# Gates multiplied straight out of the PSUM bank, norms moved to VectorE, a reciprocal built from Ln and Exp on ScalarE

## The chip, the cores and the metric

The kernel is one program on one core of a Trainium2 chip. The metric is the device time of one execution, in microseconds. Five engines work side by side, each through its own queue in order: TensorE (PE; its weight loads are listed as PEld), VectorE (DVE), ScalarE (ACT), GpSimd (POOL) and SyncE (SP), which here issues the transfers. They meet through semaphores.

## The reference

Two transformer-like layers work on `x` of shape 8 x 512 x 256. Layer 0 is a state-space block and a gated MLP, layer 1 a cumulative attention and a mixture of experts. Each of the four parts is followed by `layernorm(x + part(x))`. Cut to what matters here:

```python
# layer 0, state space: 512 channels, 128 states, one step per position
h = exp(dt_t * A) * h + dt_t * B_t * u_t ;  y_t = h . C_t
y = y * rsqrt(mean(y*y) + eps) * norm_w ;  y = y * silu(z) ;  out = y @ out_proj
# layer 0, MLP
h = silu(x@w1 * s1) * (x@w2 * s2) ; h = gelu(h@h1) ; h = gelu(h@h2) ; out = h@w3
# layer 1, attention, its input under one more rms_norm (no weight)
q, k, v = split(rms_norm(x) @ w_qkv) ; q, k = rms_norm(q), rms_norm(k)
w = cumsum(exp(k)) ; kv = cumsum(exp(k) * v)
y = sigmoid(q) * kv / (w + 1e-6) ; u, g = split(y @ w_swiglu) ; out = x + (u * silu(g)) @ w_out
# layernorm(x) = (x - mean) / sqrt(var + 1e-5)
```

## The kernel before, in words

Three phases follow one another: a projection phase (the inputs of the recurrence, written to memory), `stream_phase` (the recurrence, with all of layer 0's rest and the attention mixed in) and `expert_phase`. The change is in `stream_phase` alone.

`stream_phase` cuts the 512 positions into 8 chunks of 64 (all 8 sequences at once). Stage c, one call of `body(c, m, last)` on every engine, runs the recurrence of chunk c; beside it the engines work on chunk m = c - 1: layer 0 of that chunk and the attention of the chunk before it. Stage 0 has nothing beside the recurrence, stage 1 only layer 0. After stage 7 a tail works off the last chunk, with wider use of the banks.

The recurrence has 256 slots n = 0..255 per stage (position t = n // 4, two sequences each), paired as k = n // 2 = 0..127:

- GpSimd multiplies the state by the decay (L1612) in slot n, after VectorE's add of slot n - 4 and after the decay of k is ready.
- ScalarE makes the decay of k + 3 in its turn k (`exp_pool`, L1264, from rows that SyncE fetched) and VectorE's share of it (`exp_dve`, L1269, in place in a bank, after TensorE's L884).
- VectorE adds the input term in slot n (L1650), after GpSimd's product of slot n and TensorE's outer product (L870), and in even slots multiplies its own share (`keep`, L1640).
- TensorE waits in slot n for the add of slot n, then issues the outer product of slot n + 2, then the mixed-in product of slot n, if there is one, and after odd slots reads the state out (L896).

The mixed-in work stands in tables of slots. TensorE has one bank, `bank[:, M0]`, for all mixed-in products: each must be read before the next is written. `bank_read` waits for whoever frees the one before (`FREED_BY`). `GATE_AT` = 44, 48, .. 72 and `UP_AT` = 46, 50, .. are the eight pairs of gate and up products of the MLP, `Z_AT` = 1, 3, 5, 7 the four z products, `SWI_AT` = 174, 176, 188, 189 the four of the attention's gate.

For a gate, ScalarE copies the product out of the bank in the turn that covers its slot (`copy_gate`, L1332, with the scale s1), which frees the bank, and takes tanh of half the copy (`tanh_gate`, L1337). VectorE forms (tanh + 1) * copy three slots after the product (`silu_gate`, L1692) and multiplies it with the up product in the slot after that one (`hidden`, L1698). z (`copy_z` L1309, `tanh_z` L1313, `silu_z` L1671) and the attention's gate (`copy_swi` L1407, `tanh_swi` L1411, `silu_swi` L1748) go the same way.

For a layernorm, VectorE takes mean and variance (L1656, L1660), ScalarE the root as exp(-0.5 ln(var + eps)) (`root`, L1280 to L1283, which loads its table set explicitly each time), VectorE forms a shift (`spread`, L1665), and ScalarE applies scale and shift (`normed`, L1304), four tiles of 128 x 256. The extra rms_norm in front of the attention is made by ScalarE from the normed x: four squares (L1353), a root, four scalings (`to_unit`, L1359). The reciprocal of the attention's denominator is VectorE's (L1737), two of 128 x 512 per chunk.

VectorE and ScalarE take this work in program order with the recurrence: a mixed-in instruction that waits holds back the adds or the decays behind it.

## Time and profile before

| | |
|---|---|
| Median of the three timed runs (5382.38 to 5397.47) | 5395.41 us |
| Profiled execution, its own time | 5389.25 us |
| Its span | 5387.5 us |
| Granted TensorE clock over the span | 0.888 of full speed |
| Busy time: PE, DVE, ACT, POOL | 4718.6, 3855.4, 3391.4, 4011.9 us |
| Stages 0 to 7 of the stream (first to last L1612) | 316.8 to 4308.6 us |
| Tail of the stream | 4308.6 to 4636.5 us |

Times in the rows are microseconds from the start of the span, durations microseconds or, where marked so, nanoseconds; TensorE's busy time is modelled and says little of how near it is to its peak. Idle time of an engine is given with what released it.

### The profile page before, as it was taken

How to read it: one execution, taken by the hardware profiler on the slowest of the kernel's cores; microseconds unless marked ns; L12 is line 12 of the kernel's file. 1: busy time of each engine (PE TensorE's matmuls, PEld its weight loads, DVE VectorE, ACT ScalarE, POOL GpSimd, SP SyncE). 2: the span in 40 equal slices, each digit the busy share in tenths (PEclk: the TensorE clock that was granted, in tenths of full speed). 3: DMA queues.
4: the chain of work that ended last, by engine and by line, in shares of the span. 5: the costliest groups of instructions: out<-in, count | busy, mean ns of one | idle time of the engine just before them, and what ended most of it. 6: DMA issues, size and time to landing. Idle time of an engine off the chain costs nothing. (4 is left out here: it accounts for less than half of the span.)

```text
span 5387.5 us, 69474 instructions
## 1 busy us (share of the span) xinstructions
PE 4718.6 (88%) x21278; PEld 1827.4 (34%) x21278; DVE 3855.4 (72%) x4448; ACT 3391.4 (63%) x4022; POOL 4011.9 (74%) x2364
## 2 busy tenths in 40 slices
PE   8669998998999899989988998999899978569998
PEld 4301112223222222322222222222322334458886
DVE  6868888888988898879889987898898830500012
ACT  6646666777777877787777777777877643111112
POOL 0079998998999899989989998999899900243332
PEclk9855558998999999999999998999999989589999
DMA  3367766776777677767776776777677712245445
GB/s 112 123 212 262 246 239 227 272 263 235 253 249 271 237 256 254 270 220 251 261 263 232 264 261 243 247 261 266 242 252 265 257 51 63 77 166 179 176 176 184
DMA packets 316759, 1189.59 MB, mean 221 GB/s; under 512 B 77296, under 2 KB 115056, under 8 KB 305392
## 3 DMA queue, kind: packets, MB, share of 16 engines
q1 hardware_dynamic: 293456, 1070.18, 57.3%
q0 software_dynamic: 22944, 114.98, 6.1%
q8 instruction: 182, 2.98, 0.2%
q14 instruction: 177, 1.45, 0.1%
HBM read 1129.61 MB, written 89.19 MB: 226 GB/s over the span
## 5 line engine op out<-in xcount | busy, mean ns | idle before, releaser
L1612 POOL TENSOR_TENSOR s_h<-s_decay,s_h 128x768 f32<-128x768 f32 x2048 | 3708.8, 1852 | 282.8 <-ACT s_decay L1264 272.9
L1650 DVE TENSOR_TENSOR s_h<-s_h,bank 128x1024 f32<-128x1024 f32 x2048 | 2470.2, 1216 | 394.2 <-POOL s_h L1612 210.9
L1264 ACT ACTIVATE s_decay<-s_decay,s_a_neg 128x1536 f32<-128x1536 f32 x1024 | 1606.5, 1569 | 231.3 <-DMA s_decay<-dt_rows 229.8
L896 PE MATMUL bank<-s_h,s_cdiag 128*32 128x512 f32 x8192 | 1251.7, 687 | 10.8 <-ACT s_y L1276 10.7
L1269 ACT ACTIVATE bank<-bank,s_a_neg 128x512 f32<-128x512 f32 x1024 | 672.4, 657 | 637.3 <-PE bank L884 633.8
L870 PE MATMUL bank<-s_vrow,s_brow 9*128 9x512 bf16 x4096 | 844.6, 421 | 260.0 <-DVE s_h L1650 228.5
L870 PEld LDWEIGHTS bank<-s_vrow,s_brow 9*128 9x128 bf16 x4096 | 209.0, 92 | 1480.3 <-issue 1477.1
L1640 DVE TENSOR_TENSOR s_h<-bank,s_h 128x512 f32<-128x512 f32 x1024 | 699.8, 683 | 3.4 <-ACT bank L1269 3.1
L1008 PE MATMUL bank<-m_mb,m_w 128*128 128x512 f32 x1024 | 518.0, 635 | 1.4 <-ACT m_mb L1342 1.4
L994 PE MATMUL bank<-m_ma,m_w 128*128 128x512 f32 x1024 | 517.1, 634 | 0.0
L884 PE MATMUL bank<-s_drow,s_unit 3*128 3x512 bf16 x1024 | 432.2, 423 | 76.4 <-DMA s_drow<-dt_parts 46.9
L2204 ACT ACTIVATE e_hid<-bank 128x512 f32<-128x512 f32 x156 | 93.3, 598 | 454.2 <-PE bank L2063 454.2
L896 PEld LDWEIGHTS bank<-s_h,s_cdiag 128*32 128x32 f32 x8192 | 169.5, 114 | 403.8 <-issue 385.7
L2063 PE MATMUL bank<-e_pj,e_hid 128*128 128x256 f32 x1248 | 278.7, 381 | 12.0 <-issue 12.0
L2063 PE MATMUL bank<-e_cT,e_fc 128*128 128x256 f32 x1248 | 278.4, 382 | 0.8 <-DVE e_cT L2389 0.8
L884 PEld LDWEIGHTS bank<-s_drow,s_unit 3*128 3x128 bf16 x1024 | 96.4, 94 | 493.6 <-issue 471.1
L2063 PEld LDWEIGHTS bank<-e_pj,e_hid 128*128 128x128 f32 x1248 | 233.9, 190 | 50.5 <-issue 20.3
L2063 PEld LDWEIGHTS bank<-e_cT,e_fc 128*128 128x128 f32 x1248 | 238.9, 191 | 34.1 <-issue 1.2
L994 PEld LDWEIGHTS bank<-m_ma,m_w 128*128 128x128 f32 x1024 | 181.2, 194 | 200.6 <-issue 200.5
L1008 PEld LDWEIGHTS bank<-m_mb,m_w 128*128 128x128 f32 x1024 | 180.7, 194 | 198.1 <-issue 195.9
L2000 POOL MEMSET e_eps<- 128x1 f32 x1 | 0.1, 98 | 327.7 <-POOLq L2498 327.7
L2389 DVE COPY e_cT<-bank 128x256 f32<-128x256 f32 x39 | 16.6, 425 | 299.9 <-PE bank L2123 299.9
(229 smaller groups left out, 4096.5 us busy)
## 6 DMA issues: line engine op xcount, KB each, us to landing
s_decay<-dt_rows SPq DMA_DIRECT2D x1024, 768.0 KB, 5.6
m_w<-in_units SPq DMA_DIRECT2D x210, 512.0 KB, 5.5
s_vrow<-v_parts SPq DMA_DIRECT2D x1024, 36.0 KB
slots<-in_fill SPq DMA_DIRECT2D x512, 64.5 KB, 4.5
s_brow<-b_parts SPq DMA_DIRECT2D x1024, 9.0 KB
v_parts<-p_part SPq DMA_DIRECT2D x24, 512.0 KB, 3.0
m_w<-w_scaled SPq DMA_DIRECT2D x16, 512.0 KB, 4.9
e_got<-expert_out SPq DMA_DIRECT2D x8, 1024.0 KB, 7.1
```

What stands on the lines that cost most here:

```text
L870: mm = pe.matmul(bank[:, X0 + n % 2 * PAIR + b], brow[q:q + PAIRS, buf, hf, at * STATE:(at + 1) * STATE], vrow[q:q + PAIRS, buf, hf, at * ...
L884: pe.matmul(bank[:, E0 + hf], unit[q:q + PARTS], drow[q:q + PARTS, buf, t % STEPS], start=True, stop=True).then_inc(e_ps, 1)
L896: mm = pe.matmul(bank[q * 32:(q + 1) * 32, Y0], cdiag[:, hf * LANES + q, at * BLK:(at + 1) * BLK], h[:, t % 2, hf * LANES + q], start=(at ...
L994: mm = pe.matmul(bank[:, j % 4 if tail else M0], w[:, slot, k * P:(k + 1) * P], ma[:, k], start=(k == 0), stop=(k == KH - 1))
L1008: mm = pe.matmul(bank[:, j % 4 if tail else M0], w[:, slot, k * P:(k + 1) * P], mb[:, k], start=(k == 0), stop=(k == KH - 1))
L1264: act.activation(decay[:, k % RING], decay[:, k % RING], ACT.Exp, scale=a_neg[:, 1:2]).then_inc(decay_ok, 1)
L1269: act.activation(bank[:, E0 + k % HALVES], bank[:, E0 + k % HALVES], ACT.Exp, scale=a_neg[:, 1:2]).then_inc(e_ok, 1)
L1612: pool.tensor_tensor(h[:, t % 2, g * PAIR:(g + 1) * PAIR, DCOLS:], decay[:, k % RING, g % 2 * PAIR:(g % 2 + 1) * PAIR], h[:, (t + 1) % 2, ...
L1640: dve.tensor_tensor(h[:, t % 2, hf * LANES:(hf + 1) * LANES, 0:DCOLS], bank[:, E0 + hf].rearrange("p (b d) -> p b d", b=LANES), h[:, (t + ...
L1650: dve.tensor_tensor(h[:, t % 2, g * PAIR:(g + 1) * PAIR], h[:, t % 2, g * PAIR:(g + 1) * PAIR], bank[:, X0 + n % 2 * PAIR:X0 + (n % 2 + 1) ...
L2063: mm = pe.matmul(dst, lhs(k), rhs(k), start=(k == 0), stop=(k == n - 1))
L2204: act.activation(hid[:, r, 2 * m:2 * m + 2].rearrange("p m t -> p (m t)"), bank[:, m], ACT.Gelu).then_inc(up_ok, 1)
```

## The change

- z, gate and attention gate are no longer copied out of the bank. ScalarE takes the tanh from the bank (for the gate with scale 0.5 * s1), and VectorE forms (tanh + 1) * bank. The s1 of the copy goes into the constant of `hidden`, 0.5 * s1 * s2. The bank is now freed by VectorE's product, so `FREED_BY` names `z_ok`, `g_ok2` and `sg_ok`.
- VectorE's product stands one slot after TensorE's: `SILU_Z_AT` 2, 4, 6, 8; `SILU_GATE_AT` 45, 49, .. 73; `SILU_SWI_AT` 175, 177. Two up products move (63 to 62, 71 to 70).
- `spread`, its shift and ScalarE's `normed` go. VectorE applies (x - mean) * rstd with a tensor_scalar on four tiles per norm, at slots 36 to 39, 155 to 164 and 211 to 214.
- The four squares of the extra rms_norm go: its root is taken from the layernorm's variance, since rstd * rms of the normed x is 1 / sqrt(var * (1 + eps_rms) + eps_ln * eps_rms). `root_x` now stands ahead of `root_var` of norm 1, both in ScalarE's turn 0, and VectorE makes the unit x from the raw x (`unit_x`, slots 3 to 6).
- The two reciprocals go; ScalarE takes Ln of both denominators, then Exp of minus that (`invert`, turn 60). The denominators are formed at 112 and 116 instead of 114 and 124.
- Behind three of the sixteen Gelus the Ln-and-Exp set is loaded explicitly. The root of norm 0 moves from turn 16 to 17, that of norm 2 from 103 to 104.

```diff
-UP_AT = (46, 50, 54, 58, 63, 66, 71, 74)
+UP_AT = (46, 50, 54, 58, 62, 66, 70, 74)
...
-FREED_BY = {"z": ("z_free", TT), "xn": ("xn_ok", KD), "qk": ("qk_cp", TT), "gT": ("gT_ok", KI), "o": ("o_add", 2),
-"kT": ("ew_ok", KD), "qT": ("eq_ok", KD), "v": ("kv_ok", KD), "xt": ("xt_ok", KD), "gate": ("g_free", KH),
+FREED_BY = {"z": ("z_ok", TT), "xn": ("xn_ok", KD), "qk": ("qk_cp", TT), "gT": ("gT_ok", KI), "o": ("o_add", 2),
+"kT": ("ew_ok", KD), "qT": ("eq_ok", KD), "v": ("kv_ok", KD), "xt": ("xt_ok", KD), "gate": ("g_ok2", KH),
...
-SILU_Z_AT = (4, 5, 8, 10)
-SILU_GATE_AT = (47, 51, 55, 59, 63, 67, 71, 75)
-SILU_SWI_AT = (180, 183)
-ROOT_AT = (16, 0, 103)
-SPREAD_AT = (35, 3, 210)
-ROOT_X_AT = 2
+SILU_Z_AT = (2, 4, 6, 8)
+SILU_GATE_AT = (45, 49, 53, 57, 61, 65, 69, 73)
+SILU_SWI_AT = (175, 177)
+ROOT_AT = (17, 0, 104)
+NORM_AT = ((36, 37, 38, 39), (155, 158, 161, 164), (211, 212, 213, 214))
+UNIT_X_AT = (3, 4, 5, 6)
+LOG_NEXT = (("h1", 4), ("h2", 5), ("h2", KH - 1))
...
-DEN_AT = (114, 124)
-REC_AT = (121, 131)
+DEN_AT = (112, 116)
+INVERT_AT = 60
...
-NORM_1_AT = {2: (0, 1, 2, 3)}
-X_SQ_AT = {2: (0, 1, 2, 3)}
-TO_UNIT_AT = {2: (0,), 3: (1, 2, 3)}
...
-NORM_0_AT = {17: (0,), 18: (1, 2, 3)}
-NORM_2_AT = {106: (0,), 108: (1, 2, 3)}
...
-        pe.wait_ge(S("sg_free"), FIRST + m * KD + i - 1)
+        pe.wait_ge(S("sg_ok"), FIRST + m * KD + i - 1)
...
-def root(m, mean, dst, eps, ln_sem, ok_sem):
+def root(m, mean, dst, eps, ln_sem, ok_sem, scale=1.0):
...
-    act.activation(dst, mean, ACT.Ln, bias=eps).then_inc(ln_sem, 1)
+    act.activation(dst, mean, ACT.Ln, bias=eps, scale=scale).then_inc(ln_sem, 1)
...
 def root_x(m):
-    act.wait_ge(S("xsq"), FIRST + (m + 1) * TT)
-    root(m, sm[:, 8:12], sm[:, 12:16], eps_rms, S("xrs_ln"), S("xrs_ok"))
+    act.wait_ge(S("mv_ok", 1), FIRST + (m + 1) * TT)
+    root(m, mv[:, 1, :, 1], sm[:, 12:16], eps_both, S("xrs_ln"), S("xrs_ok"), 1.0 + RMS_EPS)
...
 def root_qk(m):
-def normed(m, n, i, src, dst):
-    act.wait_ge(S("sh_ok", n), FIRST + m + 1)
-    act.activation(dst[:, i], src[:, i], ACT.Identity, scale=rstd[:, n, i:i + 1],
-                   bias=shift[:, n, i:i + 1]).then_inc(S("lnx", n), 1)
-def copy_z(m, i, tail):
+def tanh_z(m, i, tail):
...
-    act.activation(sz[:, i], bank[:, i if tail else M0], ACT.Copy).then_inc(S("z_free"), 1)
-def tanh_z(m, i):
-    act.wait_ge(S("z_free"), FIRST + m * TT + i + 1)
-    act.activation(ma[:, KI + i], sz[:, i], ACT.Tanh, scale=0.5).then_inc(S("z_th"), 1)
+    act.activation(ma[:, KI + i], bank[:, i if tail else M0], ACT.Tanh, scale=0.5).then_inc(S("z_th"), 1)
...
-def mean_square_x(m, i):
-    act.wait_ge(S("lnx", 1), FIRST + m * TT + i + 1)
-    act.activation(xn2[:, i], x2[:, i], ACT.Square, scale=DIM ** -0.5, accum_out=sm[:, 8 + i:9 + i]).then_inc(S("xsq"), 1)
-def to_unit(m, i):
-    if i == 0:
-        act.wait_ge(S("xrs_ok"), FIRST + m + 1)
-        act.wait_ge(S("out_ok"), FIRST + m)
-    act.activation(xn2[:, i], x2[:, i], ACT.Identity, scale=sm[:, 12 + i:13 + i]
-                   ).then_inc(S("xr_ok"), 1)
...
-def copy_swi(m, i, tail):
+def invert(m):
+    act.preload_act_table_set("natural_log_exp_and_others")
+    for c in range(KD):
+        act.wait_ge(S("den_ok"), FIRST + m * KD + c + 1)
+        act.activation(data(qk_runs[:, c]), data(qk_runs[:, c]), ACT.Ln).then_inc(S("rec_ln"), 1)
+    for c in range(KD):
+        act.wait_ge(S("rec_ln"), FIRST + m * KD + c + 1)
+        act.activation(data(qk_runs[:, c]), data(qk_runs[:, c]), ACT.Exp, scale=-1.0).then_inc(S("rec_ok"), 1)
+def tanh_swi(m, i, tail):
...
-    act.activation(u[:, i], bank[:, 4 + i if tail else M0], ACT.Copy).then_inc(S("sg_free"), 1)
-def tanh_swi(m, i):
-    act.wait_ge(S("sg_free"), FIRST + m * KD + i + 1)
-    act.activation(qk[:, i], u[:, i], ACT.Tanh, scale=0.5).then_inc(S("sg_th"), 1)
+    act.activation(qk[:, i], bank[:, 4 + i if tail else M0], ACT.Tanh, scale=0.5).then_inc(S("sg_th"), 1)
...
 def out_of_bank(m, n, attn):
-        copy_z(m, Z_AT.index(n), False)
-        tanh_z(m, Z_AT.index(n))
+        tanh_z(m, Z_AT.index(n), False)
...
-        copy_gate(m, GATE_AT.index(n), False)
-        tanh_gate(m, GATE_AT.index(n))
+        tanh_gate(m, GATE_AT.index(n), False)
...
-        copy_swi(m - 1, SWI_AT.index(n), False)
-        tanh_swi(m - 1, SWI_AT.index(n))
+        tanh_swi(m - 1, SWI_AT.index(n), False)
...
+            if ("h1", j) in LOG_NEXT:
+                act.preload_act_table_set("natural_log_exp_and_others")
...
+            if ("h2", j) in LOG_NEXT:
+                act.preload_act_table_set("natural_log_exp_and_others")
...
 def aside(m, k, attn):
+        root_x(m - 1)
...
-    if attn and k in NORM_1_AT:
-        for i in NORM_1_AT[k]:
-            normed(m - 1, 1, i, x2, x2)
-    if attn and k in X_SQ_AT:
-        for i in X_SQ_AT[k]:
-            mean_square_x(m - 1, i)
-    if attn and k == ROOT_X_AT:
-        root_x(m - 1)
-    if attn and k in TO_UNIT_AT:
-        for i in TO_UNIT_AT[k]:
-            to_unit(m - 1, i)
...
-    if k in NORM_0_AT:
-        for i in NORM_0_AT[k]:
-            normed(m, 0, i, xa, xa)
-    if attn and k in NORM_2_AT:
-        for i in NORM_2_AT[k]:
-            normed(m - 1, 2, i, x2, xn2)
+    if attn and k == INVERT_AT:
+        invert(m - 1)
...
-def spread(m, n):
+def normed(m, n, i, src, dst):
...
-    dve.scalar_tensor_tensor(out=shift[:, n], in0=mv[:, n, :, 0], scalar=-1.0, in1=rstd[:, n], op0=ALU.mult,
-                             op1=ALU.mult).then_inc(S("sh_ok", n), 1)
-def silu_z(m, i):
+    if n == 1:
+        dve.wait_ge(S("xr_ok"), FIRST + (m + 1) * TT)
+    if n == 2 and i == 0:
+        dve.wait_ge(S("out_ok"), FIRST + m)
+    dve.tensor_scalar(dst[:, i], src[:, i], mv[:, n, i, 0:1], rstd[:, n, i:i + 1], ALU.subtract, ALU.mult
+                      ).then_inc(S("lnx", n), 1)
+def unit_x(m, i):
+    if i == 0:
+        dve.wait_ge(S("xrs_ok"), FIRST + m + 1)
+        dve.wait_ge(S("out_ok"), FIRST + m)
+    dve.tensor_scalar(xn2[:, i], x2[:, i], mv[:, 1, i, 0:1], sm[:, 12 + i:13 + i], ALU.subtract, ALU.mult
+                      ).then_inc(S("xr_ok"), 1)
+def silu_z(m, i, tail):
...
-    dve.scalar_tensor_tensor(out=sz[:, i], in0=ma[:, KI + i], scalar=1.0, in1=sz[:, i],
+    dve.scalar_tensor_tensor(out=sz[:, i], in0=ma[:, KI + i], scalar=1.0, in1=bank[:, i if tail else M0],
...
-def silu_gate(m, j):
+def silu_gate(m, j, tail):
...
-    dve.scalar_tensor_tensor(out=mb[:, j], in0=ma[:, j], scalar=1.0, in1=mb[:, j], op0=ALU.add,
-                             op1=ALU.mult).then_inc(S("g_ok2"), 1)
+    dve.scalar_tensor_tensor(out=mb[:, j], in0=ma[:, j], scalar=1.0, in1=bank[:, j % 2 * 2 if tail else M0],
+                             op0=ALU.add, op1=ALU.mult).then_inc(S("g_ok2"), 1)
...
 def hidden(m, j, tail):
-                             scalar=half_s2[:, j:j + 1], in1=mb[:, j], op0=ALU.mult, op1=ALU.mult
+                             scalar=half_s12[:, j:j + 1], in1=mb[:, j], op0=ALU.mult, op1=ALU.mult
...
 def add_attended(m, pair, tail):
+    dve.wait_ge(S("lnx", 1), FIRST + (m + 1) * TT)
...
 def mix(m, n, attn):
-    if attn and n == SPREAD_AT[1]:
-        spread(m - 1, 1)
...
-        silu_z(m, SILU_Z_AT.index(n))
+        silu_z(m, SILU_Z_AT.index(n), False)
+    if attn and n in UNIT_X_AT:
+        unit_x(m - 1, UNIT_X_AT.index(n))
...
-    if n == SPREAD_AT[0]:
-        spread(m, 0)
+    if n in NORM_AT[0]:
+        normed(m, 0, NORM_AT[0].index(n), xa, xa)
+    if attn and n in NORM_AT[1]:
+        normed(m - 1, 1, NORM_AT[1].index(n), x2, x2)
...
-        silu_gate(m, SILU_GATE_AT.index(n))
+        silu_gate(m, SILU_GATE_AT.index(n), False)
...
-for i in range(TT):
-    normed(end, 0, i, xa, xa)
...
+invert(end - 1)
...
-    copy_gate(end, j, True)
-    tanh_gate(end, j)
+    tanh_gate(end, j, True)
...
-for i in range(TT):
-    normed(end - 1, 2, i, x2, xn2)
...
+root_x(end)
...
-for i in range(TT):
-    normed(end, 1, i, x2, x2)
-for i in range(TT):
-    mean_square_x(end, i)
...
+invert(end)
...
-for i in range(TT):
-    normed(end, 2, i, x2, xn2)
...
```

## Rows read from the trace of the kernel before

**Rows 1.** page, costliest groups: count, busy us, mean ns, idle before them us and its releasers

```profile
L1612 POOL TENSOR_TENSOR s_h<-s_decay,s_h 128x768 f32<-128x768 f32 x2048 | 3708.8, 1852 | 282.8 <-ACT s_decay L1264 272.9
L1650 DVE TENSOR_TENSOR s_h<-s_h,bank 128x1024 f32<-128x1024 f32 x2048 | 2470.2, 1216 | 394.2 <-POOL s_h L1612 210.9
```

**Rows 2.** groups by line, GpSimd alone: stage 0 (316.8 to 773.1), stage 6 (3301.1 to 3807.2)

```profile
L1612 POOL TENSOR_TENSOR s_h<-s_decay,s_h 128x768 f32<-128x768 f32 x256 | 455.6, 1825 | 0.7 <-ACT s_decay L1264 0.4
...
L1612 POOL TENSOR_TENSOR s_h<-s_decay,s_h 128x768 f32<-128x768 f32 x257 | 467.8, 1857 | 40.1 <-ACT s_decay L1264 39.6 <-DVE s_h L1650 0.3
```

**Rows 3.** timeline around one gate: start us, duration us, instruction, idle before it

```profile
3422.63 1.21 DVE L1650 TENSOR_TENSOR s_h<-s_h,bank 128x1024 f32<-128x1024 f32 x1
3423.99 0.39 PE L870 MATMUL bank<-s_vrow,s_brow 9*128 9x512 bf16 x2 [0.82 <-DVE s_h L1650]
3424.31 1.98 PE L970 MATMUL bank<-m_cT,m_w 128*128 128x512 f32 x4
3426.33 0.69 ACT L1332 ACTIVATE m_mb<-bank,m_s 128x512 f32<-128x512 f32 x1 [1.98 <-PE bank L970]
3427.05 0.63 ACT L1337 ACTIVATE m_ma<-m_mb 128x512 f32<-128x512 f32 x1
3427.86 1.98 PE L980 MATMUL bank<-m_cT,m_w 128*128 128x512 f32 x4
3428.34 1.80 DVE L1692 SCALAR_TENSOR_TENSOR m_mb<-m_ma,m_mb 128x512 f32<-128x512 f32 x1
3430.18 0.75 DVE L1698 SCALAR_TENSOR_TENSOR m_ma<-bank,m_half_s,m_mb 128x512 f32<-128x512 f32 x1
3430.84 1.21 DVE L1650 TENSOR_TENSOR s_h<-s_h,bank 128x1024 f32<-128x1024 f32 x1
3432.52 1.98 PE L970 MATMUL bank<-m_cT,m_w 128*128 128x512 f32 x4
```

**Rows 4.** windows: all eight gates, busy us by engine, granted clock, DMA

```profile
3408.03:3472.16 64.13, 57.81 (x273) 16.63 (x273) 60.62 (x64) 45.85 (x52) 56.75 (x32) 1.00 0.69 238
```

**Rows 5.** groups by line and shape, whole trace: the fused multiply on two kinds of operands

```profile
L1748 DVE SCALAR_TENSOR_TENSOR m_u<-m_qk,m_u 128x512 f32<-128x512 f32 x16 | 27.6, 1728 | 9.9 <-ACT m_qk L1411 9.9
L1759 DVE SCALAR_TENSOR_TENSOR m_x<-m_x,bank 128x512 f32<-128x512 f32 x16 | 11.0, 687 | 14.9 <-PE bank L1103 14.9
```

**Rows 6.** timeline, opening of stage 6: table load, root, first tanh, GpSimd's stall

```profile
3310.12 1.21 DVE L1650 TENSOR_TENSOR s_h<-s_h,bank 128x1024 f32<-128x1024 f32 x1
3310.87 1.28 ACT L1280 ACT_TABLE_LOAD   x1
3312.17 0.30 ACT L1281 ACTIVATE m_rstd<-m_mv,m_const 128x4 f32<-128x4 f32 x1
3315.11 0.63 ACT L1313 ACTIVATE m_ma<-m_mb 128x512 f32<-128x512 f32 x1
...
3333.35 1.82 POOL L1612 TENSOR_TENSOR s_h<-s_decay,s_h 128x768 f32<-128x768 f32 x1 [7.84 <-ACT s_decay L1264]
```

**Rows 7.** timeline, VectorE, where the first norm's shift is formed

```profile
3389.80 0.16 DVE L1665 SCALAR_TENSOR_TENSOR m_shift<-m_mv,m_rstd 128x4 f32<-128x4 f32 x1 [0.64 <-ACT m_rstd L1283]
3391.65 1.21 DVE L1650 TENSOR_TENSOR s_h<-s_h,bank 128x1024 f32<-128x1024 f32 x1
```

**Rows 8.** groups by line and shape: VectorE's tensor_scalar elsewhere in this trace

```profile
L370 DVE TENSOR_SCALAR p_conv<-p_xpad,p_cw,p_cb 128x512 f32<-128x512 f32 x16 | 8.7, 542 | 19.6 <-ACT p_xpad L280 19.6
L2344 DVE TENSOR_SCALAR e_parts<-e_job,e_jobs,e_more 128x40 f32<-128x40 f32 x7 | 2.1, 306 | 0.0
```

**Rows 9.** timeline: a reciprocal in the stream and the two of the tail

```profile
3556.75 3.35 DVE L1737 RECIPROCAL m_qk<-m_qk 128x512 f32<-128x512 f32 x1
...
4381.75 6.55 DVE L1737 RECIPROCAL m_qk<-m_qk 128x512 f32<-128x512 f32 x2
```

**Rows 10.** timeline, ScalarE, the tail's opening

```profile
4320.80 1.28 ACT L1280 ACT_TABLE_LOAD   x1
4332.70 1.71 ACT L1359 ACTIVATE m_xn<-m_x,m_sm 128x256 f32<-128x256 f32 x4
```

More of the change, by code:

```diff
@@ L1837, in keys_tail @@
                 for c in range(KD):
-                    invert(m, c)
-                for c in range(KD):
                     divide(m, c)
@@ L1843, in output_tail @@
                 for c in range(KD):
-                    silu_swi(m, c)
+                    silu_swi(m, c, True)
                 for c in range(KD):
@@ L1862, in _ @@
                 statistics(end, 0, xa, S("o_add"), pair)
-            spread(end, 0)
+            for i in range(TT):
+                normed(end, 0, i, xa, xa)
             keys_tail(end - 1)
             for j in range(KH):
-                silu_gate(end, j)
+                silu_gate(end, j, True)
                 hidden(end, j, True)
@@ L1872, in _ @@
                 statistics(end, 1, x2, S("x2_ok"), pair)
-            spread(end, 1)
+            for i in range(TT):
+                unit_x(end, i)
+            for i in range(TT):
+                normed(end, 1, i, x2, x2)
             keys_tail(end)
```

79 lines of the change are left out of this document (35 added, 44 removed).

## The prediction

> **What bounds the kernel now.** I read the costliest groups first, then GpSimd stage by stage, then the timeline of one stage, instruction by instruction. The stream is GpSimd's chain of decays: 2048 products of 1.85 us [rows 1]. Stage 0, which has only the recurrence, takes 256 slots in 456.3 us, 1.78 us a slot, with next to no idle time; stage 6 takes 506.1 us for as many, with 40.1 us idle, 39.6 of it behind ScalarE's decays, and products lengthened from 1825 to 1857 ns, 257 x 0.032 = 8.2 us [rows 2]. So a stage with everything in it has some 50 us to win, seven stages (37 in stage 1) about 340. The lengthening comes when VectorE runs an instruction with two SBUF inputs: (tanh + 1) * copy takes 1728 ns in the mean where the same shape with one operand in a bank takes 687 [rows 5], and a GpSimd product beside it grows too.
>
> The other half of the reading is how far the chain can lean on the rest. GpSimd in slot n needs VectorE's add of slot n - 4. TensorE in slot n needs the add of slot n, and VectorE issues its adds and its mixed-in work in one order. So whatever makes VectorE wait between add n and add n + 1 also holds TensorE's product of n + 1. GpSimd runs on for at most three more slots, 5.35 us. A wait that recurs uses that up once and then costs its full length.
>
> **The gates, the largest term.** Eight gates take 64.13 us from the first to the product behind the last [rows 4], 8.02 per four slots. One round [rows 3]: add ends 3423.84, gate product 3424.31 to 3426.29, copy, tanh to 3427.68. Meanwhile VectorE adds freely, TensorE starts up at 3427.86, ends at 3429.84, VectorE multiplies (L1692, then L1698 at 3430.18), adds at 3430.84, and the next gate starts at 3432.52. Copy, tanh and L1692 lie beside the next two adds and the up product. After the change L1692 stands right behind the add of the next slot, takes its operand from tanh and must run before the add that lets TensorE start up. The round is then one chain: 0.47 from add to product, 1.98 product, 0.04, 0.69 tanh (as the copy, also out of the bank with a pointer scale), 0.04, 0.69 L1692 [rows 5], an add of 1.21 less 0.08 overlap, 0.47, 1.98 up, 0.1, 0.75 L1698, 1.21 less 0.08. Sum 9.47, against 8.02: 1.45 lost per gate, 8 x 1.45 = 11.6 us a stage. The table load ahead of the first tanh (1.28) moves ahead of its wait for TensorE, under the product: nothing. The slack of 5.35 us doesn't pay it: in this stage GpSimd is some 3 us ahead when the last round ends, and the first Gelu behind it, whose decay comes late from ScalarE, takes the lead back to the same level whatever it was. I take 11.6; the bounds are 0 (something I miss lets the adds run on) and 13.
>
> **The stage's opening.** Before, ScalarE's turn 2 holds four normed, four squares, a root and a scaling, and GpSimd stands 7.84 us [rows 6]; with the smaller stalls around it the first 16 slots lose 12.6 us. All of that work leaves ScalarE. But VectorE's product of the first z moves from slot 4 to 2, and ScalarE's queue in front of that tanh is now: two roots (each 1.28 load, 0.30, 0.20 and gaps, 1.9), a square 0.6, a load 1.3, the tanh 0.6. Counted from 3310.87 [rows 6] it ends at 3317.1. The add that ran at 3310.12 then runs at 3317.8, and GpSimd's eighth product waits for it till 3319.1, 5.4 us later than before. Three more z rounds are chains as the gates are: 0.47 + 1.98 + 0.6 + 0.7 + 0.4 (unit_x) + 1.2, some 5.5 us per two slots where GpSimd needs 3.6, less what lead there is. Worked through slot by slot, GpSimd's product 16 starts at 3340.9, before at 3342.4. I take 1 us saved, bounds 9.5 saved (only ScalarE counts) and 4 lost.
>
> **Norm 0.** The first normed on VectorE stands at slot 36 and waits for a root that moved one turn later. Before, VectorE waited 0.64 for its shift and the next-but-one add ran at 3391.65 [rows 7]. ScalarE would end the root at about 3393.2, so that add slips by 2.2 us, of which some is caught up before the first gate. Take 1.4 lost, bounds 0 and 3.
>
> **The new tensor_scalars.** Sixteen of 128 x 256 a stage. The nearest rows are 542 ns for 128 x 512 and 306 for 128 x 40 [rows 8]; between them I take 0.42. Three spreads (up to 0.97 in this stage, behind a GpSimd product) and two reciprocals of 3.35 [rows 9] leave VectorE, so its total falls. For GpSimd, fourteen two-input instructions go, about 2.3 of the 8.2 us a stage; each new one may hold it for between 0 and 0.42, I take 0.2, 3.2 us. Net 0.9 lost, bounds 2.3 won and 4.4 lost.
>
> The Trainium skill (SBUF — State Buffer, Who interferes with whom) says that a VectorE instruction with two SBUF inputs, or a tensor_scalar in a two-port mode, holds the port pair it shares with GpSimd, and the second to start fully blocks. The 1728 against 687 ns agree for the first kind; no row shows the second beside GpSimd, and by that rule it costs the whole bound of 0.42.
>
> **Reciprocals and invert.** A reciprocal delays one add by 3.35 us and TensorE's piece behind it by about 1.4 us, and the Gelu stalls that follow lose 0.4 to 0.9 each. ScalarE gets 3.8 us in turn 60 (a load and four instructions of 0.6), of which its slack of some 3 us and the free 1.5 us a turn hide all but 0.3. Net 1 saved, bounds 2 saved and 1.5 lost. Table loads per stage stay 41: one less at z, one more at invert, three explicit ones in place of three implicit.
>
> **Attention's gate and norm 2.** Slots 174 and 176 are two more chained rounds. VectorE's product there no longer takes 2.34 and 1.87 us later on, so most is caught up by slot 184, but TensorE's pieces slip by about 1.6 us into a Gelu that already stalls. 1.6 lost, bounds 0 and 4. ScalarE's four normed of norm 2 gone: 0.7 saved, bounds 0 and 1.5.
>
> **The tail.** Nothing covers it, so what leaves the chain counts. ScalarE's copies and tanhs of z ran ahead of a root at 4320.80, four normed, four squares, and the extra root, and the scalings at 4332.70 [rows 10]; now both norm roots go under the z products and unit_x runs beside the rest: the first turned x comes 10.8 us earlier. At the end chunk the same again in serial, 6. The reciprocals were 6.55 each time [rows 9]; a load, which can go ahead, and Ln and Exp of 0.6 overlapping leave 2.8 and 4 saved. Copies ahead of tanh and the last spread and normed: 2.4. Sum 26 saved, bounds 12 and 32.
>
> **Sum.** A full stage: 11.6 - 1 + 1.4 + 0.9 - 1 + 1.6 - 0.7 = 12.8 lost, six of them 77. Stage 1 (no attention): 11.6 less 2 of z work, about 10. Tail -26. Together +61 on the profiled execution's 5389.25, 5450. The runs' median of 5395.41 stands 6 above that execution: 5456.
>
> **The rivals.** (1) The lead covers the chained rounds and only ScalarE's load counts. For it: 39.6 of 40.1 us of idle time are put down to ScalarE. Against it: in [rows 4] VectorE is busy 60.62 of 64.13 us and GpSimd only 56.75, so there it is no longer GpSimd that sets the pace. Per stage 9.5 at the opening, 8 x 0.6 at the gates (the copy), 1 at the reciprocals, 1 at each of the last two: 17 saved, six times, 8 in stage 1, 26 in the tail: 5259. It decides if VectorE's wait for tanh is under the time to its next add, 0.1 us, and I count 1.4. (2) The rounds cost half of 1.45 because up or the adds overlap more than one trace shows, and the opening saves 4: 5456 - 7 x 5.8 - 6 x 3 = 5397, no change. (3) The tensor_scalars hold GpSimd for their whole 0.42 and VectorE waits for the product that runs, up to 1.8 each, so that norm 0 and the unit_x round lose another 3: 3.5 + 3 per stage, six times 39: 5495. It decides where VectorE's own lead is gone, as at slots 36 to 39. (2) and the forecast differ in size, (1) in sign. The rule of the Trainium skill quoted above would put (3) at its full price.
>
> **How the numbers follow.** Forecast 0.66, rival (1) 0.13, (2) 0.11, (3) 0.10. The likeliest case alone spans 5415 to 5485. The range that leaves 2 in 10 out runs from 5385, inside rival (2), to 5500. A measurement here tells about 0.3%, 16 us, from no change. Faster: (1) and a corner of (2), 0.15; same: most of (2), 0.10; slower 0.75.
>
> **What would show it.** Right: the distance from one gate's first product to the next is 9.3 to 9.7 us; VectorE's L1692 counterpart shows idle time behind tanh; TensorE's outer products wait more for VectorE; GpSimd's idle time moves from ScalarE's decays to VectorE's adds and grows in slots 50 to 80; full stages take some 519 us; the tail is 300 us long. Wrong: rounds of 8 us or less there (the gate step falls), no stall near slot 7 or 8 (the opening), tensor_scalars with a mean over 1 us or GpSimd's mean over 1.87 (the locks).

## The result, and the profile after

The changed kernel takes 5589.51 us (median of 4 runs, 5582.65 to 5597.83) against 5388.90 us of the kernel before beside it (5380.50 to 5397.47): 1.037 times as long, 95% interval 1.0347 to 1.0392. The direction was forecast, the size was not: 61 us more were forecast, 201 came. The profiled execution took 5597.83 us, the longest of the four; its granted clock was 0.873 where it had been 0.888.

The page's costliest groups answer [rows 1] (count, busy us, mean ns, idle before them):

```profile
L1561 POOL TENSOR_TENSOR s_h<-s_decay,s_h 128x768 f32<-128x768 f32 x2048 | 3702.3, 1843 | 521.2 <-ACT s_decay L1260 389.4
L866 PE MATMUL bank<-s_vrow,s_brow 9*128 9x512 bf16 x4096 | 862.3, 428 | 437.7 <-DVE s_h L1601 406.9
```

GpSimd works as long as before, its products are even a little shorter, but it stands idle 521.2 us instead of 282.8: the whole loss is waiting. Half of the growth is put down to ScalarE's decays (272.9 to 389.4 us), half to VectorE's adds (8.7 to 125.4 us). GpSimd alone, grouped by line, in stages 0 and 6 [rows 2]:

```profile
L1561 POOL TENSOR_TENSOR s_h<-s_decay,s_h 128x768 f32<-128x768 f32 x257 | 457.3, 1825 | 2.0 <-ACT s_decay L1260 1.1 <-PE bank L892 0.8
...
L1561 POOL TENSOR_TENSOR s_h<-s_decay,s_h 128x768 f32<-128x768 f32 x258 | 468.9, 1851 | 67.2 <-ACT s_decay L1260 49.3 <-DVE s_h L1601 16.6 <-PE bank L892 0.8
```

Stage 3 cut at slots 0, 16, 44, 80, 136, 172 and 256, first the kernel before, then the changed one. The columns are the stretch and its length, busy us (count) of PE, PEld, DVE, ACT and POOL, the granted clock, DMA share, GB/s:

```profile
1775.86:1816.76 40.90, 30.23 (x125) 7.71 (x117) 29.80 (x31) 37.47 (x62) 29.10 (x18) 0.75 0.67 238
1816.76:1872.91 56.15, 49.36 (x275) 18.74 (x273) 48.74 (x58) 48.61 (x78) 51.61 (x28) 0.97 0.69 232
1872.91:1944.71 71.80, 64.70 (x309) 18.99 (x307) 67.26 (x71) 51.33 (x61) 65.06 (x38) 1.00 0.69 243
1944.71:2057.03 112.32, 102.18 (x471) 28.46 (x470) 104.37 (x94) 81.20 (x80) 103.26 (x57) 0.94 0.73 253
2057.03:2124.08 67.05, 63.13 (x302) 18.23 (x301) 57.75 (x58) 52.47 (x52) 65.14 (x37) 1.00 0.76 259
2124.08:2281.53 157.45, 146.00 (x727) 48.00 (x726) 136.78 (x151) 115.36 (x120) 150.83 (x85) 0.98 0.78 267
```

```profile
1829.69:1871.20 41.51, 31.53 (x124) 7.44 (x123) 26.47 (x33) 29.07 (x41) 28.84 (x18) 0.71 0.63 228
1871.20:1933.97 62.77, 54.77 (x259) 19.93 (x259) 50.72 (x60) 47.09 (x73) 51.63 (x28) 0.83 0.64 214
1933.97:2026.28 92.31, 72.93 (x324) 21.14 (x323) 64.67 (x74) 46.58 (x52) 64.72 (x38) 0.94 0.56 197
2026.28:2134.20 107.92, 102.05 (x475) 28.82 (x473) 97.14 (x93) 85.11 (x85) 104.68 (x57) 0.97 0.75 257
2134.20:2209.60 75.40, 66.34 (x299) 18.40 (x298) 66.55 (x61) 52.15 (x52) 64.90 (x38) 0.91 0.69 237
2209.60:2371.48 161.88, 148.15 (x724) 48.35 (x723) 133.88 (x153) 111.25 (x113) 150.11 (x85) 0.95 0.76 258
```

Slots 44 to 80, the gates, lose 20.5 us; slots 16 to 44 lose 6.6 and slots 136 to 172 lose 8.4. The granted clock is lower in each of the stretches that lengthened.

This cut, made for every kernel of the study, is how the parts were told apart. The table (its kernels are described with the experiments) gives the time that GpSimd's slots took over 1.784 us each, as a mean of stages 2 to 7, worked out from the starts of its products; the last column is the median of the timed runs (the kernel before had 5384 to 5391 us beside the different groups of kernels):

| kernel | 0-16 | 16-44 | 44-80 | 80-136 | 136-172 | 172-212 | 212-256 | sum | median us |
|---|---|---|---|---|---|---|---|---|---|
| before | 12.8 | 7.1 | 8.1 | 11.0 | 2.6 | 5.1 | 3.6 | 50.2 | 5387 |
| changed | 14.0 | 9.8 | 28.6 | 11.2 | 7.5 | 6.7 | 7.8 | 85.7 | 5590 |
| gates_only | 12.5 | 6.4 | 26.0 | 12.4 | 3.0 | 4.3 | 3.8 | 68.5 | 5514 |
| gates_back | 15.0 | 11.0 | 11.6 | 10.8 | 5.4 | 7.0 | 6.1 | 66.8 | 5478 |
| bank_back | 11.8 | 8.0 | 11.4 | 11.9 | 8.4 | 6.0 | 7.3 | 64.7 | 5447 |
| z_only | 20.3 | 5.2 | 8.0 | 10.9 | 2.8 | 4.5 | 3.6 | 55.2 | 5422 |
| recip_back | 11.7 | 7.6 | 11.9 | 12.3 | 4.4 | 4.7 | 7.4 | 60.0 | 5431 |
| norm0 | 12.0 | 6.7 | 7.9 | 11.9 | 3.7 | 5.0 | 7.6 | 54.8 | 5397 |
| guard2 | 12.1 | 7.2 | 11.2 | 12.4 | 4.2 | 4.8 | 7.1 | 59.0 | 5418 |
| tail_only | 12.7 | 7.2 | 7.9 | 9.6 | 2.7 | 4.5 | 4.4 | 49.0 | 5361 |
| guard | 15.6 | 8.3 | 28.3 | 12.9 | 5.6 | 7.2 | 7.0 | 84.9 | 5588 |
| tuned | 11.6 | 7.4 | 11.2 | 13.5 | 6.2 | 5.9 | 4.6 | 60.4 | 5400 |
| fill | 14.3 | 6.6 | 28.8 | 12.8 | 5.3 | 7.3 | 7.5 | 82.7 | 5586 |
| heavy | 15.0 | 8.5 | 31.8 | 11.9 | 6.2 | 7.0 | 7.6 | 88.0 | 5615 |

Behind the last product of stage 7 the changed kernel needs 1053.7 us to the end of its span (5596.0 - 4542.3), the kernel before 1078.9 (5387.5 - 4308.6).

**The gate round** [rows 3], timeline of stage 6 (start us, duration us, instruction, idle before it):

```profile
3585.28 1.21 DVE L1601 TENSOR_TENSOR s_h<-s_h,bank 128x1024 f32<-128x1024 f32 x1
3585.53 1.98 PE L966 MATMUL bank<-m_cT,m_w 128*128 128x512 f32 x4
3587.56 0.69 ACT L1318 ACTIVATE m_ma<-bank,m_half_s 128x512 f32<-128x512 f32 x1 [2.27 <-PE bank L966]
3588.28 0.69 DVE L1655 SCALAR_TENSOR_TENSOR m_mb<-m_ma,bank 128x512 f32<-128x512 f32 x1 [1.78 <-ACT m_ma L1318]
3588.88 1.21 DVE L1601 TENSOR_TENSOR s_h<-s_h,bank 128x1024 f32<-128x1024 f32 x1
3590.24 0.39 PE L866 MATMUL bank<-s_vrow,s_brow 9*128 9x512 bf16 x2 [1.40 <-DVE s_h L1601]
3590.56 2.93 PE L976 MATMUL bank<-m_cT,m_w 128*128 128x512 f32 x3
```

It is the chain that the prediction wrote down, down to 3590.56 us. Then comes what it didn't have: the up product takes 3.7 us instead of 1.98 (the row shows three of its four parts). The windows show why (a round with it, its two parts, the round behind it):

```profile
3585.54:3596.68 11.14, 8.93 (x36) 2.60 (x35) 6.84 (x8) 4.82 (x5) 7.04 (x4) 0.85 0.55 191
...
3585.54:3590.50 4.96, 3.56 (x19) 1.05 (x17) 3.18 (x4) 2.73 (x3) 3.55 (x3) 1.00 0.43 144
3590.50:3594.20 3.70, 3.70 (x9) 1.22 (x7) 1.32 (x2) 0.00 (x0) 3.49 (x2) 0.54 0.56 214
...
3596.68:3606.14 9.46, 7.24 (x36) 2.11 (x34) 7.15 (x9) 4.87 (x6) 7.21 (x4) 1.00 0.37 136
```

At full clock a round is 9.46 us, 9.47 were forecast. But TensorE is busy only 3.56 of the 4.96 us in front of 3590.5, and then its granted clock is at the lower level, 1.2 GHz instead of 2.4. Two to four rounds a stage cost 1.1 to 1.7 us more that way: 22 of the 49 distances of stages 1 to 7 are over 10.8 us, 22 are 9.46. The gaps are the same in the rounds that stay at 1.00, so what decides between them isn't shown. [rows 4] had 1.00 over all eight gates.

### The profile page after: what moved, and what is told of

Its sections match the earlier page's. It is cut to its first block and busy times, and to the rows that moved or that the text cites. A ratio compares the mean times of both kernels' runs of the same rounds, so it can differ in the third digit from the quotient of the medians.

```text
span 5596.0 us, 69345 instructions
## 1 busy us (share of the span) xinstructions
PE 4815.5 (86%) x21278; PEld 1846.5 (33%) x21278; DVE 3845.0 (69%) x4537; ACT 3272.6 (58%) x3753; POOL 4005.3 (72%) x2365
## 5 line engine op out<-in xcount | busy, mean ns | idle before, releaser
L1561 POOL TENSOR_TENSOR s_h<-s_decay,s_h 128x768 f32<-128x768 f32 x2048 | 3702.3, 1843 | 521.2 <-ACT s_decay L1260 389.4
L892 PE MATMUL bank<-s_h,s_cdiag 128*32 128x512 f32 x8192 | 1275.0, 699 | 9.4 <-ACT s_y L1272 9.4
L866 PE MATMUL bank<-s_vrow,s_brow 9*128 9x512 bf16 x4096 | 862.3, 428 | 437.7 <-DVE s_h L1601 406.9
L880 PEld LDWEIGHTS bank<-s_drow,s_unit 3*128 3x128 bf16 x1024 | 96.8, 95 | 521.2 <-issue 496.9
L2029 PEld LDWEIGHTS bank<-e_pj,e_hid 128*128 128x128 f32 x1248 | 233.9, 190 | 50.5 <-issue 20.3
L1976 POOL DMA_INDIRECT e_pj<-in_pj,e_rows x39 | 37.5, 961 | 255.9 <-PE bank L2029 247.4
```

What stands on the lines that cost most here:

```text
L866: mm = pe.matmul(bank[:, X0 + n % 2 * PAIR + b], brow[q:q + PAIRS, buf, hf, at * STATE:(at + 1) * STATE], vrow[q:q + PAIRS, buf, hf, at * ...
L880: pe.matmul(bank[:, E0 + hf], unit[q:q + PARTS], drow[q:q + PARTS, buf, t % STEPS], start=True, stop=True).then_inc(e_ps, 1)
L892: mm = pe.matmul(bank[q * 32:(q + 1) * 32, Y0], cdiag[:, hf * LANES + q, at * BLK:(at + 1) * BLK], h[:, t % 2, hf * LANES + q], start=(at ...
L1561: pool.tensor_tensor(h[:, t % 2, g * PAIR:(g + 1) * PAIR, DCOLS:], decay[:, k % RING, g % 2 * PAIR:(g % 2 + 1) * PAIR], h[:, (t + 1) % 2, ...
L2029: mm = pe.matmul(dst, lhs(k), rhs(k), start=(k == 0), stop=(k == n - 1))
```

## Experiments

**The gates, undone in the changed kernel and alone in the kernel before.**

```diff
+# gates_back; gates_only is the reverse of it, in the kernel before
+act.activation(mb[:, j], bank[..], ACT.Identity, scale=k_["s1"][:, j:j + 1]).then_inc(S("g_free"), 1)
+act.wait_ge(S("g_free"), FIRST + m * KH + j + 1)
+act.activation(ma[:, j], mb[:, j], ACT.Tanh, scale=0.5).then_inc(S("g_th"), 1)
...
-UP_AT = (46, 50, 54, 58, 62, 66, 70, 74)
+UP_AT = (46, 50, 54, 58, 63, 66, 71, 74)
...
-SILU_GATE_AT = (45, 49, 53, 57, 61, 65, 69, 73)
+SILU_GATE_AT = (47, 51, 55, 59, 63, 67, 71, 75)
```

> The changed kernel with one part undone: the gates are copied out of the bank again, tanh and VectorE's product read the copy, in their old slots; the scale of the up product is s2 / 2 again. Theory A (the chained rounds, and a lower granted clock of TensorE that follows from its gaps in them): the 36 slots from 44 to 80 lost 28.6 us a full stage in the changed kernel and 8.1 in the kernel before; all 20.5 come back in six stages and 16.3 in stage 1, and the granted clock of these slots is 1.00 again: 5590 - 139 = 5450 us. Theory B (only the 1.45 us of each chained round is the gates', what is above it comes from the new VectorE instructions or the transfers and stays): 8 x 1.45 x 7 = 81, so 5509 us, with single rounds of over 10 us left.

> The kernel before with this one part of the change alone: the gates multiplied out of the bank. Theory A: as much as it gives back in the changed kernel, 5389 + 139 = 5528 us, rounds of 9.46 us with about three in eight of over 11 at a granted clock near 0.85. Theory B: rounds of 9.46 alone, 5389 + 81 = 5470 us.

5478.39 us (1.0156 times the kernel before, 1.0126 to 1.0186): 111 us come back. Alone, 5513.58 us (1.0238, 1.0214 to 1.0261): 123 us more. Both lie between the theories, the first halfway, the second nearer to A. Slots 44 to 80 give back 17.0 of the 20.5 us; 3.5 stay and belong to something else. The seven distances between the first and the last gate of stage 6 sum to 56.1 us in gates_back and in the kernel before, to 72.3 in the changed one and to 71.9 in gates_only.

**Is it the clock?** Two kernels give TensorE more to do in the rounds.

```diff
 # fill: the same product in front, 2 times; heavy: two full fp32 products in front
+for _ in range(2 if m is not None and 44 <= n < 76 else 0):
+    pe.matmul(bank[:, E0 + hf], k_["ident"][:], mask[:, 0:BANK], start=True, stop=True)
 pe.matmul(bank[:, E0 + hf], unit[q:q + PARTS], drow[q:q + PARTS, buf, t % STEPS], ...)
```

> The changed kernel with more work for TensorE: from slot 44 to 75 each product that spreads the rows of VectorE's decays is issued three times into the same bank, the last one counts (some 0.33 us more each time, 1.3 us per gate round, where TensorE stands 2.2 us). Nothing else changes, the result is the same. Theory A (the rounds of 11.1 us are rounds in which the granted clock of TensorE fell after gaps): with the gaps filled the clock of slots 44 to 80 stays near 1.00, rounds of 9.46 us throughout, 3 x 1.65 us less in each of seven stages: 5590 - 35 = 5555 us. Rival (the slow rounds come from the transfers or from VectorE's ports, and the clock in the records only goes along): rounds of over 11 us remain and the time is the same or, with TensorE later by 0.3 us here and there, up to 20 us longer.

> The changed kernel with more work for TensorE than in the run with the rows issued three times: from slot 44 to 75 two whole products of 128 x 128 by 128 x 512 in fp32 stand ahead of each spreading of rows, into the bank that this then overwrites (some 0.43 us each at the higher clock). The lighter filling took the rounds of over 10.8 us of each stage from three to one or two, but not away, and moved the time by nothing. Theory A (the clock falls because TensorE does too little in the chained rounds): no round over 10.8 us, the seven distances between gates sum to 67 us instead of 72: 5590 - 35 = 5555 us. Rival (the clock falls for another reason than these gaps): one to three such rounds a stage remain; with up to 0.2 us lost where the filling delays an outer product, 5590 to 5610 us.

fill: 5586.22 us, no gain; in every stage one to three rounds still take over 10.7 us, though in three stages the sum of the seven distances, which was 72.1 to 73.6 us, is about 69. heavy: 5614.89 us (1.0434). All its rounds of stage 6 are the same, and the granted clock is 1.00; the first line is the stretch of seven distances, the second one round:

```profile
3584.76:3658.63 73.87, 73.87 (x295) 25.04 (x295) 50.22 (x57) 35.66 (x37) 49.75 (x28) 1.00 0.53 187
3595.33:3605.87 10.54, 10.54 (x45) 3.57 (x43) 7.15 (x9) 4.99 (x6) 7.17 (x4) 1.00 0.49 167
```

So theory A is right on the cause and was wrong on the price of the cure. With TensorE busy all the time 48 of the 49 rounds have a granted clock of 1.00 (the first of stage 1 has 0.94), though VectorE's instructions are the same and the transfers nearly so. But the filling sits on the chain: each round is 1.08 us longer, which is more than the clock cost. What the clock costs is read from stage 5 of the guard run below, in which the gaps were there and it stayed at 1.00 all the same: its seven distances sum to 67.42 us, against 72.27 in stage 6 of the changed kernel. That is 4.9 us a stage; the chain alone is 67.4 - 56.1 = 11.3.

The Trainium skill (TensorE: Matmul & The Clock Gate, A second HAM failure mode: psum-queue depth-cycling) tells of a kernel in which short idle times between groups of matmuls made the clock go up and down. The rows agree: the gaps here are of 0.81 to 1.40 us each.

**All three products off the bank, and z alone.**

```diff
+# bank_back: copy_z and copy_swi as copy_gate above; z_only is the reverse for z, in the kernel before
-SILU_Z_AT = (2, 4, 6, 8)
+SILU_Z_AT = (4, 5, 8, 10)
-SILU_SWI_AT = (175, 177)
+SILU_SWI_AT = (180, 183)
```

> The changed kernel with all three products out of the bank undone (the gates, z and the attention's gate); the norms by VectorE, the root from one variance, the reciprocals on ScalarE and the early table loads stay. Theory A (the chains through the one bank are what costs; the rest is worth what was forecast): the gates' 139, at the opening some 9 us a full stage because only ScalarE's relief is left there, 3 at the attention's gate: 5590 - 139 - 6 x 12 = 5379 us, near or below the kernel before. Theory B (VectorE's new tensor_scalars cost the stream several us a stage themselves): at or above 5420 us.

> The kernel before with this one part of the change alone: z is multiplied out of the bank, tanh reads it there, VectorE's product stands at slots 2, 4, 6 and 8; ScalarE keeps the four norms, the four squares and the scalings of its turn 2. In the changed kernel with the gates undone, undoing z as well took slots 4 to 34 from 22.3 to 16.7 us above 1.784 us a slot. Theory (z's four chained rounds cost by themselves): 5.6 x 6 = 34 us, 5421 us. Rival (in the kernel before the chain lies behind ScalarE's full turn, on which GpSimd waits 7.8 us anyway): slots 4 to 34 stay within 1 us of 17.1, 5387 to 5393 us. Or the two add up, since tanh now waits in the same queue behind that turn and the bank is not free until VectorE has run: over 5430 us.

bank_back: 5446.77 us (1.0099, 1.0072 to 1.0127), 32 less than gates_back; 5379 were expected. z_only: 5421.58 us (1.0075, 1.0048 to 1.0102), 37 more than before by the medians and 26 between the profiled executions: 7.5 a stage in slots 0 to 16, of which 1.9 come back by slot 44. So z costs a stage 5 to 6 us. In the changed kernel its first round looks like this:

```profile
3482.19 0.60 ACT L1299 ACTIVATE m_ma<-bank 128x512 f32<-128x512 f32 x1
3482.82 0.69 DVE L1634 SCALAR_TENSOR_TENSOR m_mb<-m_ma,bank 128x512 f32<-128x512 f32 x1 [6.55 <-ACT m_ma L1299]
...
3484.72 3.68 POOL L1561 TENSOR_TENSOR s_h<-s_decay,s_h 128x768 f32<-128x768 f32 x2 [5.32 <-DVE s_h L1601]
```

What theory A missed in bank_back: taking the norms, squares and scalings off ScalarE's turn 2 shortens slots 0 to 16 by 1.0 us, not by nine. The stall of 7.84 us [rows 6] goes, and VectorE's waits for the root (1.41 us in stage 3) and for z's tanh (1.77 and 1.65 us) put others in its place.

**The reciprocals.**

```diff
+# recip_back: bank_back, and the reciprocals again on VectorE
+dve.reciprocal(data(cw(c)), data(cw(c))).then_inc(S("rec_ok"), 1)   # slots 121, 131
-invert(m - 1)                                                       # ScalarE, turn 60
-DEN_AT = (112, 116)
+DEN_AT = (114, 124)
-LOG_NEXT = (("h1", 4), ("h2", 5), ("h2", KH - 1))
+LOG_NEXT = (("h2", 5), ("h2", KH - 1))
```

> The changed kernel with the three products out of the bank undone and the reciprocals back on VectorE too; the norms by VectorE and the root from one variance remain, with the tail that goes with them. Theory (as forecast, the reciprocals on ScalarE are worth about 1 us a stage and 8 in the tail; but they give GpSimd a lead with which it shuts the division of slot 141 out, 6.45 us in five of six stages): slots 112 to 136 get 1 us longer, slots 136 to 172 fall from 8.4 to some 4 us above 1.784 us a slot; 5447 + 6 - 26 + 8 = 5435 us. Rival (it is the norms' tensor_scalars at slots 155 to 164 that cost there): slots 136 to 172 stay at 8 us, 5460 us.

5430.82 us (1.0083, 1.0052 to 1.0114), 16 less than bank_back; the four runs of each just touch (5418 to 5436 and 5433 to 5457). In the stream the reciprocals on ScalarE, with the denominators and the table load that go with them, cost 4.7 us a stage by the traces, nearly all in slots 136 to 172, where no reciprocal stands. There the changed kernel's timeline of stage 7 shows (VectorE, GpSimd, TensorE):

```profile
4316.16 6.46 DVE L1701 SCALAR_TENSOR_TENSOR m_u<-m_qk 128x512 f32<-128x512 f32 x1
...
4297.11 24.97 POOL L1561 TENSOR_TENSOR s_h<-s_decay,s_h 128x768 f32<-128x768 f32 x14 [0.35 <-ACT s_decay L1260]
4323.83 3.58 POOL L1561 TENSOR_TENSOR s_h<-s_decay,s_h 128x768 f32<-128x768 f32 x2 [1.76 <-DVE s_h L1601]
4330.89 3.60 POOL L1561 TENSOR_TENSOR s_h<-s_decay,s_h 128x768 f32<-128x768 f32 x2 [3.48 <-ACT s_decay L1260]
...
4324.20 0.61 PE L866 MATMUL bank<-s_vrow,s_brow 9*128 9x512 bf16 x2 [5.99 <-DVE s_h L1601]
4324.74 3.51 PE L990 MATMUL bank<-m_ma,m_w 128*128 128x512 f32 x4
```

VectorE's division reads two operands from SBUF. Issued at 4316.16 us it ends at 4322.62, half a microsecond after GpSimd's unbroken row of 14 products ends at 4322.08. Alone it takes 1.1 us, so it waits over five; GpSimd goes on for three more products, as far as its lead over VectorE's adds carries it. Then the lead is gone, TensorE has stood 5.99 us, and its product runs at half speed (granted clock 0.56). This happens in four of six full stages of the changed kernel, in five of bank_back and in none of recip_back, where the division takes 1.06 us. Nor does it happen in any other kernel that has its reciprocals on VectorE in the stream (before, gates_only, z_only, norm0, tail_only: 1.05 to 1.09 us each time). That fits reciprocals which use up GpSimd's lead in slots 121 and 131, but no run separates this. The kernel before does it to a scan, in three stages (6.40, 6.41 and 7.01 us):

```profile
2494.97 7.01 DVE L1726 TENSOR_TENSOR_SCAN m_qk<-m_mask,m_u 128x520 f32<-128x520 f32 x1
...
2473.23 27.66 POOL L1612 TENSOR_TENSOR s_h<-s_decay,s_h 128x768 f32<-128x768 f32 x15
```

This is the exception. Of the 69 instructions with two SBUF inputs that in the changed kernel's stream were issued in an unbroken row of GpSimd's products, 62 came through behind the one that was running; the other seven, four divisions and three scans, were held over three more. All seven were issued 0.6 us before the running product ended, but five others with the same 0.6 us were not held, so the cause stays open. The division of slot 149, in stage 7 too, in a row that goes on:

```profile
4336.55 2.16 DVE L1701 SCALAR_TENSOR_TENSOR m_u<-m_qk 128x512 f32<-128x512 f32 x1
...
4336.35 9.40 POOL L1561 TENSOR_TENSOR s_h<-s_decay,s_h 128x768 f32<-128x768 f32 x5 [1.87 <-ACT s_decay L1260]
```

**Keeping GpSimd out.**

```diff
+# guard: in the changed kernel, d = 4; guard2: in bank_back, d = 2
+if c >= 2 and n - d in DIV_AT:
+    pool.wait_ge(S("yc_ok"), FIRST + (c - 2) * KD + DIV_AT.index(n - d) + 1)
 pool.tensor_tensor(h[...], decay[...], h[...], ALU.mult).then_inc(pool_kept, 1)
```

> The changed kernel with one wait added: GpSimd's product of slot 145 waits for VectorE's division of slot 141, that of slot 153 for the division of slot 149 (nothing is left out). In the changed kernel's trace the first division takes 6.45 us in four of six full stages (1.1 to 2.2 otherwise), while GpSimd's products run one behind the other, and ends as GpSimd has nothing left to do; GpSimd then stands 1.8 + 3.5 to 4.0 us at slots 145 and 147. Theory (VectorE's instruction with two SBUF inputs gets the shared port only when GpSimd stops): the division takes 1.1 to 1.3 us in all stages, the two stalls go, some 5 us in four stages and 1 lost for the wait in each: 5590 - 15 = 5575 us, slots 136 to 172 from 7.5 to about 4 us above 1.784 us a slot. Rival (the division waits for something else, for instance ScalarE's exponential or a transfer): it still takes over 6 us, and the time is the same or longer.

> The changed kernel with the three products out of the bank undone (5447 us), and GpSimd's wait for the two divisions two slots behind them: its products of slots 143 and 151 wait for VectorE's divisions of slots 141 and 149. In the run with the wait four slots behind, the shut-out division took 4.70 us instead of 6.45, which is one GpSimd product less. Theory (the division runs when GpSimd stops, wherever that is): it takes 1.1 to 1.8 us in all stages instead of 6.46 in five of six, slots 136 to 172 fall from 8.4 to some 4 us above 1.784 us a slot: 5447 - 26 = 5421 us. Rival (its length hangs on something that only went along with GpSimd's slots): over 4 us in some stages, and 5440 us or more.

guard: 5587.79 us, no gain that can be measured, and the division takes not 1.1 to 1.3 but 4.70 us in three stages. guard2: 5418.32 us (1.0066, 1.0045 to 1.0087), 28 less than bank_back, and 1.14 to 1.17 us in all six. VectorE and GpSimd in stage 7, guard first, then guard2:

```profile
4308.92 4.70 DVE L1703 SCALAR_TENSOR_TENSOR m_u<-m_qk 128x512 f32<-128x512 f32 x1
...
4293.44 19.64 POOL L1563 TENSOR_TENSOR s_h<-s_decay,s_h 128x768 f32<-128x768 f32 x11
4313.79 5.35 POOL L1563 TENSOR_TENSOR s_h<-s_decay,s_h 128x768 f32<-128x768 f32 x3 [0.72 <-DVE m_u L1703]
```

```profile
4139.47 1.15 DVE L1720 SCALAR_TENSOR_TENSOR m_u<-m_qk 128x512 f32<-128x512 f32 x1
...
4123.99 16.07 POOL L1581 TENSOR_TENSOR s_h<-s_decay,s_h 128x768 f32<-128x768 f32 x9
4140.79 5.40 POOL L1581 TENSOR_TENSOR s_h<-s_decay,s_h 128x768 f32<-128x768 f32 x3 [0.72 <-DVE m_u L1720]
```

Once it is held, the division's end follows the slot at which GpSimd is made to stop: one product earlier, 1.76 us shorter; three, and it runs right behind the running product. An added wait makes the kernel faster. The Trainium skill (SBUF — State Buffer, Who interferes with whom), quoted in the prediction, agrees that the second to start waits for the whole instruction, and says that the order of issue decides. The runs show more: in these cases products that GpSimd starts after the division was issued go first as well.

**Norm 0, and moving the norms.**

```diff
+# norm0: recip_back, and norm 0 again with its spread (slot 35) and ScalarE's scaling (turns 17, 18)
-ROOT_AT = (17, 0, 104)
+ROOT_AT = (16, 0, 104)
+# tuned: bank_back with guard's wait, and
+ROOT_AT = (16, 0, 103)
+NORM_AT = (.., .., (214, 215, 216, 217))
+UNIT_X_AT = (5, 6, 7, 8)
```

> As the run with the three products out of the bank and the reciprocals undone (5431 us), and norm 0 back on ScalarE as well, with its spread on VectorE and its root one turn earlier: of the norms only 1 and 2 stay on VectorE. That run lost 11.9 us from slot 44 to 80 a full stage and 7.8 from 80 to 112, the kernel before 8.1 and 5.7. Theory (the late gates there come from norm 0's tensor_scalars and their later root): back to about 8.5 and 6 in six stages and 3 less in stage 1, 5431 - 36 = 5395 us; the tail gets 2 longer. Rival (they come from GpSimd's and VectorE's changed leads): less than half of it, 5415 us or more.

> The changed kernel with the three products out of the bank undone, with GpSimd's wait for the two divisions, and with VectorE's norms moved behind their roots: the unit scalings from slots 3 to 6 to slots 5 to 8, norm 2 from 211 to 214, its root and that of norm 0 one turn earlier, as they were before the change. In the trace of the kernel without these moves VectorE stood 1.05 us for the root at slot 3 and 2.56 us at slot 211, and the first tensor_scalar behind it took 1.12 and 2.18 us, before a GpSimd stall of 4.3 and 3.5 us. Theory: slots 4 to 16 from 11.8 to 8, 34 to 80 from 14.6 to 12, 136 to 172 from 8.4 to 4, 212 to 256 from 7.3 to 4 us above 1.784 us a slot, 13 us in six stages: 5447 - 78 = 5370 us, 20 under the kernel before. Rival (the new order only moves the waits to the next late link): less than half of it, 5410 us or more.

norm0: 5397.36 us (1.0025, 1.0007 to 1.0043): norm 0 on VectorE costs 33 us, 4.0 a stage in slots 44 to 80. All of that falls in slots 44 to 52 (6.9 in recip_back, 2.7 here); the seven distances between the gates of stage 6 sum to 56.1 us in both. tuned: 5400.02 us (1.0019, 0.9996 to 1.0041; ten runs, 5374.60 to 5425.79, of which the profiled one took 5425.09), 47 us less than bank_back; 77 were expected. Of its moves that of norm 2 did what it should: slots 212 to 256 fall from 7.3 to 4.6. The moved scalings left slots 0 to 16 at 11.6, and its wait stands four slots behind the division, as in guard, so that the division still takes 4.7 us in four stages.

tuned also tells the two parts of norm 0 apart. With the root one turn earlier VectorE no longer waits for it in slot 36 (2.23 us or more in every full stage of bank_back), and slots 36 to 44 fall from 3.2 to 2.3. But slots 44 to 80 stay at 11.2 after 11.4. What norm0 lacks and tuned, recip_back and bank_back have in every full stage is a wait of ScalarE: its copy of the turned, normed x stands 3.3 to 5.0 us for TensorE's L951, with decays behind it. Stage 5, tuned first, then norm0 (there L1326, without a wait):

```profile
2914.37 0.60 ACT L1318 ACTIVATE m_cT<-bank 128x512 f32<-128x512 f32 x1 [3.31 <-PE bank L951]
...
2897.42 0.58 ACT L1326 ACTIVATE m_cT<-bank 128x512 f32<-128x512 f32 x1
```

**The tail alone.**

```diff
+# the kernel before; behind the last slot of the stream, the changed kernel's attention_tail, keys_tail,
+# output_tail and the lines between them, with tanh, products, norms, unit_x and invert as it has them
```

> The kernel before up to the last slot of the stream, and from there the changed kernel's order: z, gates and the attention's gate multiplied out of their banks (each has one of its own there), the norms by VectorE, the root of x from the variance, the reciprocals on ScalarE. Between the two kernels what lies outside the eight stages fell by 25.2 us (1078.9 to 1053.7). Theory (the parts are independent; the change is a gain where GpSimd runs no longer and no bank is shared): 5387 - 25 = 5362 us, faster than both. Rival (the last stage's lead, or the state in which the stream leaves the engines, took part in it): 5375 us or more.

5360.55 us (12 runs, 5349.93 to 5382.08): 0.996 times the kernel before, interval 0.9945 to 0.9974, faster than both. From the last product of the stream to the end of the span 1052.0 us pass (5349.7 - 4297.7). The unit x, 24.1 us behind the stream's end before (4332.70 in [rows 10], less 4308.6), comes 8.0 us behind it here and in the changed kernel, whose row this is:

```profile
4550.33 1.38 DVE L1628 TENSOR_SCALAR m_xn<-m_x,m_mv,m_sm 128x256 f32<-128x256 f32 x4 [4.79 <-ACT m_sm L1279]
```

## Why the prediction was right in sign and wrong in size

Undoing part after part leads from the changed kernel back to the one before: gates 111, z and the attention's gate 32, reciprocals 16, norm 0 33, and the rest (with the tail's gain in it) some 9, 201 in all. By the prediction's steps, per full stage:

- **Gates, 11.6 forecast.** The chain was right: 9.46 us a round, 11.3 for the seven distances where 7 x 1.45 = 10.2 were forecast. The step that failed is that it took TensorE's durations from a stretch at full clock and kept them after adding gaps. The clock costs 4.9 more, seven times 34 us. The bound of 13 was too low for the same reason: 17.0 measured.
- **Opening, -1 forecast.** The chained z rounds were there, and the stall, forecast at 5.4 us, was 5.32. Measured for slots 0 to 16 is +1.2, and +2.7 for 16 to 44. The mis-sized term is the relief: the working let ScalarE's freed turn pay for all of z's chains and leave 1 us, and alone it is worth 1.0 (bank_back).
- **Norm 0, 1.4 forecast, bounds 0 and 3.** 5.2 by recip_back against norm0. The step priced only VectorE's wait for the root. That wait came (2.23 us), but without it slots 44 to 80 stay where they are (tuned). The term left out is that the normed x is ready later on VectorE: ScalarE's copy of it waits 3.3 to 5.0 us a stage. That this wait makes the whole loss of slots 44 to 52 is argued, not shown.
- **Tensor_scalars, 0.42 each and 0.2 for GpSimd.** Alone they take 0.41 (L1628 in the changed kernel) and GpSimd's mean fell to 1843 ns. But beside a running product of GpSimd they take longer: norm 1's four in stage 6 take 1.13, 1.32, 1.49 and 0.89 us (mean 1210 ns), and of norm 2's four the first takes 1.97:

```profile
L1620 DVE TENSOR_SCALAR m_x<-m_x,m_mv,m_rstd 128x256 f32<-128x256 f32 x4 | 4.8, 1210 | 0.0
L1620 DVE TENSOR_SCALAR m_xn<-m_x,m_mv,m_rstd 128x256 f32<-128x256 f32 x4 | 3.2, 791 | 2.6 <-ACT m_rstd L1279 2.6
```

- **Reciprocals, 1 saved forecast, bounds 2 saved and 1.5 lost.** 4.7 lost. The step summed what leaves VectorE and what ScalarE takes on. It left out that VectorE's next instruction on the shared port, the division, can be shut out. The trace before had the sign of it, the scan of 7.01 us, and no row of the prediction showed it.
- **Norm 2, 0.7 saved forecast.** Slots 212 to 256 lose 4.2: VectorE reaches the first norm before the root is there (2.6 us in the row above). Moved behind its root, in tuned, it gives 2.7 back.
- **Attention's gate, 1.6 forecast.** Slots 172 to 212: +1.6, but undoing it (with z) gives only 1.0 back there, so that the number fits is in part luck. **Tail, -26 forecast.** -25.2 by the spans, -26.8 by tail_only.

Forecast 12.8 a stage, measured 35.5 (85.7 less 50.2); stage 1 lost 17.5 where 10 was forecast. Six times 22.7 and 7.5 make 144 us, and that is the miss (208.6 us between the two profiled executions, 61 forecast). The 22.7 are gates 5.4, opening 2.2, norm 0 3.8, reciprocals 5.7 and norm 2 4.9, 22.0 in sum; they were measured in different kernels, so the sum could have fitted less well. Of the signs named ahead, the waits behind tanh and for VectorE and the tail (302 us) came as said, the gate round (9.3 to 9.7) in 22 of 49 cases. GpSimd's idle time didn't move from ScalarE's decays to VectorE's adds, it grew behind both. A full stage took 532.5 to 549.5 us, not 519, and tensor_scalars reached a mean over 1 us, which had been named as a sign of rival (3). That rival had VectorE waiting for GpSimd's running product, which is right, but it had it at norm 0 and at unit_x, where the tensor_scalars mostly took 0.41 us, and not at norms 1 and 2 or the division, and for one product, not three.

What stays open: in which stages the division is shut out, and in which rounds the clock falls, differs from kernel to kernel, and no run shows what decides it.

## What to carry to other kernels

When a wait is put into a chain, ask what its gap does to the engines beside it: durations read from a busy stretch don't hold for TensorE in one with gaps. Freed time on an engine that shares a port with another can turn into that engine's waiting; a wait that stops the faster one for a microsecond may be worth several. And cut a trace into the same stretches for every experiment: a part here cost nearly the same taken out of one kernel as put into the other (gates 111 and 123 us; z with the attention's gate 32 out, z alone 37 in), and the one that paid, the tail, could be kept alone.

## What the hardware showed that was not expected

- VectorE's instruction with two SBUF operands, issued in a row of GpSimd products, came through behind the running one in 62 of 69 cases of the changed kernel, but in seven only when GpSimd stopped, three products later: 6.46 us instead of 1.15, 4.70 with the row one product shorter (guard), and 7.01 us for a scan in the kernel before.
- TensorE's granted clock fell to the lower level behind stretches in which it was busy 3.56 of 4.96 us, with single gaps of no more than 1.4 us, and a product of 1.98 us took 3.7. In other rounds with the same gaps it stayed at 1.00. With the gaps filled by full fp32 products it was 1.00 in 48 of 49 rounds; with shorter products of three rows it still fell.
